# Four x tiles in the last context group, two query tiles taken singly, and V rounded in the order 3, 0, 1, 2

## What is computed

```python
q = (x @ Wq + bq)                      # x: layernormed, 1024 rows of 512; 16 heads of 32
kv = (cond @ Wkv + bkv)                # cond: 2048 rows of context
q = _fq_sym(q * scale, axis=-1)        # round(q / s) * s, s = max|q| / 127 per row and head
k = _fq_sym(k, axis=-1)
v = _fq_sym(v, axis=2)                 # s over all 2048 rows, per column: needs every context row
attn = softmax(einsum('bhqd,bhkd->bhqk', q, k))
attn = _fq_unsigned(attn, axis=-1)     # round(attn / s) * s, s = max / 255 per row
x = x + einsum('bhqk,bhkd->bhqd', attn, v) @ Wp + bp
x = x + experts(_layernorm(x))         # gate, up, down products of 8 experts
```

## Time and profile before

| | |
|---|---|
| median of 3 runs | 724.86 us |
| the profiled execution | 726.75 us, span of its instructions 724.9 us |
| granted TensorE clock, mean | 0.987 |
| DVE busy | 569.8 us, 79% |
| PE busy | 617.2 us, 85% |
| ACT busy | 462.4 us, 64% |
| POOL busy | 402.9 us, 56% |

### The profile page before, as it was taken

The page is one execution under the profiler, slowest core; times in us unless marked ns, Lnnn a source line. Parts: engine busy times, 40 slices in busy tenths (PEclk is TensorE's granted clock), DMA queues, the critical chain, the costliest instruction groups (busy, mean ns, idle before and its releaser), DMA issues.

```text
span 724.9 us, 16059 instructions
## 1 busy us (share of the span) xinstructions
PE 617.2 (85%) x5448; PEld 333.6 (46%) x5448; DVE 569.8 (79%) x927; ACT 462.4 (64%) x561; POOL 402.9 (56%) x455
## 2 busy tenths in 40 slices
PE   6999998566767777777777787799999999999995
PEld 3744444233434334443434355455555555555543
DVE  5998887999999999999999998794746547464430
ACT  5445359789979989898989896343434434353421
POOL 4164457637587878787878773315334454334503
PEclk9999999999999999999999998899999999999998
DMA  7877867999989999999999997258696797968624
GB/s 248 203 146 174 184 136 137 180 199 189 175 166 198 184 195 193 188 193 189 191 192 185 195 183 159 88 187 224 176 249 157 221 190 200 242 163 233 139 32 58
DMA packets 318517, 129.44 MB, mean 179 GB/s; under 512 B 293508, under 2 KB 293508, under 8 KB 318472
## 3 DMA queue, kind: packets, MB, share of 16 engines
q1 hardware_dynamic: 311296, 112.64, 72.6%
q0 software_dynamic: 7168, 16.26, 10.7%
q10 hardware_dynamic: 8, 0.01, 0.0%
HBM read 44.33 MB, written 12.06 MB: 78 GB/s over the span
## 4 chain that ended last, share of the span: by engine, by line
PE 38%; issue 20%; DVE 15%; POOL 8%; DMA 7%; ACT 6%; SPq 3%; POOLq 1%; another core or an unknown queue 0%; ACTq 0%; DVEq 0%
PE psum L1690 34%; DMA work<-work 6%; DVE spare L1422 5%; ACT work L1078 4%; DVE spare L1413 4%; POOL values_region L603 2%; POOL work L672 2%; SPq L481 2%; PE psum L1867 1%; POOL resid L610 1%; SPq L450 1%; PE psum L2015 1%; SPq L483 1%; POOL out_dram L846 1%; DMA token_region<-values_region 1%
## 5 line engine op out<-in xcount | busy, mean ns | idle before, releaser
L1078 ACT ACTIVATE work<-spare,exp_bias 128x2048 uint8<-128x2048 f32 (+1 forms) x127 | 253.2, 1996 | 28.3 <-POOL exp_bias L678 20.6
L1422 DVE TENSOR_SCALAR_CACHE_REDUCE spare<-psum,q_step_now 128x1024 f32<-128x1024 f32 x128 | 162.5, 1274 | 2.0 <-PE psum L1867 1.9
L672 POOL CAST work<-work 128x2048 int16<-128x2048 uint8 x70 | 132.4, 1892 | 37.9 <-DMA work<-work 33.9
L1413 DVE TENSOR_SCALAR_CACHE_REDUCE spare<-psum,q_step_now 128x2048 f32<-128x2048 f32 x64 | 150.3, 2348 | 0.1
L1867 PE MATMUL psum<-keys_region,work 128*128 128x512 f16 x256 | 72.7, 383 | 47.3 <-DVE spare L1422 27.6
L834 POOL DMA_INDIRECT work<-x_rows,slot_tok x32 | 50.9, 1591 | 86.5 <-DVE slot_w L1622 73.2
L1867 PE MATMUL psum<-keys_region,bias_hl 128*128 128x512 f16 x256 | 70.4, 381 | 28.0 <-DVE spare L1422 22.4
L846 POOL DMA_INDIRECT out_dram<-keys_region,slot_tok x32 | 51.7, 1616 | 74.7 <-ACT keys_region L1173 67.7
L1826 PEld LDWEIGHTS psum<-values_region,work 128*128 128x128 f16 x2016 | 64.8, 96 | 34.3 <-POOL work L672 20.3
L1690 PE MATMUL psum<-work,spare 128*128 128x480 f16 (+1 forms) x396 | 79.9, 362 | 0.0
L1690 PE MATMUL psum<-work,keys_region 128*128 128x480 f16 x384 | 78.9, 366 | 0.0
(11 more groups left out here) (250 smaller groups left out, 1010.4 us busy)
## 6 DMA issues: line engine op xcount, KB each, us to landing
spare<-in_L_ffn_Wd_dram SPq DMA_DIRECT2D x8, 1024.0 KB, 15.4
spare<-in_L_ffn_Wg_dram SPq DMA_DIRECT2D x7, 1024.0 KB
spare<-in_L_ffn_Wu_dram SPq DMA_DIRECT2D x7, 1024.0 KB, 10.1
work<-in_ctx_dram SPq DMA_DIRECT2D x3, 1024.0 KB, 5.8
work<-work SPq DMA_TRANSPOSE x174, 3.7
token_region<-in_L_xattn_Wkv_dram SPq DMA_DIRECT2D x2, 1024.0 KB, 7.7
resid<-in_x_dram SPq DMA_DIRECT2D x2, 1024.0 KB, 8.4
out_dram<-work SPq DMA_DIRECT2D x8, 256.0 KB, 2.6
```

What stands on the lines that cost most here:

```text
L672: nc.gpsimd.tensor_copy(p_T_int[h % 4], pair_bytes[h % 4]).then_inc(unpacked, 1)
L1078: nc.scalar.activation(p_out, scores, ACT.Exp, bias=exp_bias[:, h % 4:h % 4 + 1], scale=-1.0, accum_out=p_sum[:, h:h + 1]).then_inc(exp_do ...
L1413: nc.vector.tensor_scalar(staged[h % 4], psum[:, at:at + 4, :].rearrange("p b k -> p (b k)"), q_step_now[:, h:h + 1], None, ALU.mult, ALU.min,
L1422: nc.vector.tensor_scalar(staged[h % 4][:, 1024 * c:1024 * c + 1024], psum[:, at:at + 2, :].rearrange("p b k -> p (b k)"), q_step_now[:, h ...
```

## The change

Tiles 4 to 7 of x are now all normalised, cut and turned within the last context group, one for each key tile, alternating with the key tiles on ACT, POOL and SP. Query tiles 0 and 1 are taken by DVE singly. V's slices are rounded in the order 3, 0, 1, 2, the first two are halved by DVE and the last two by POOL, and folding the projection weights is moved behind the rounding and, for three of four columns, behind the first exponential. PE makes head 0's scores behind the fifth query product (tile 4), and the products of tiles 5 and 6 follow, that of tile 7 behind the scores of head 1. DVE stages head 0, and takes tiles 4, 5 and 6 behind it, tile 7 ahead of head 2. The `staged` buffers of the first four heads are given in another order (`FIRST_STAGED`), so that head 0 lies over V's slice 3 and head 1 over slice 2.

The diff, cut to its core:

```diff
@@ -47,6 +47,8 @@
...
+ROUNDED = (3, 0, 1, 2)
+FIRST_STAGED = (0, 2, 1, 3)
@@ -376,7 +381,9 @@
...
-                if i >= 2:
+                    if i >= KT // 2 - 2:
+                        transpose_x(2 * i + b - QT)
+                if 2 <= i < KT // 2 - 2:
@@ -409,26 +416,22 @@
...
-                if i == DK - 1:
-                    sp.wait_ge(v_rounded, DK + 1)
-                else:
-                    sp.wait_ge(v_halved, i + 1)
+                sp.wait_ge(v_halved, ROUNDED.index(i) + 1)
...
-            transpose_x(QT - 2)
-            transpose_queries(0)
-            transpose_x(QT - 1)
-            transpose_queries(1)
+            transpose_queries(0, (0,))
...
-            transpose_values(0)
-            transpose_values(1)
-            transpose_queries(2)
-            transpose_values(2)
+            transpose_values(ROUNDED[0])
+            transpose_values(ROUNDED[1])
+            transpose_queries(0, (1,))
+            transpose_values(ROUNDED[2])
+            transpose_values(ROUNDED[3])
+            transpose_queries(1)
@@ -482,9 +485,9 @@
...
-                        transpose_values(DK - 1)
-                    if first and h in (3, 4):
-                        transpose_queries(DK - 1, range(h - 3, h - 2))
+                        transpose_queries(2)
+                    if first and h < 2:
+                        transpose_queries(DK - 1, (h,))
@@ -722,10 +726,18 @@
...
+            def halve_values(n):
+                pool.wait_ge(v_rounded, n + 1)
+                pool.wait_ge(v_halved, n)
+                nc.gpsimd.tensor_copy(v_T_int[:, ROUNDED[n], :], v_i16[:, ROUNDED[n], :]).then_inc(v_halved, 1)
+
...
+            pool.wait_ge(k_cut_ready[1], KT // 2)
+            clear_queries(own, 0)
...
-            clear_queries(own, 0)
...
+            halve_values(2)
+            halve_values(3)
@@ -950,14 +966,17 @@
...
+                    if not b and not following:
+                        rows_of_x(DK + t)
...
-                    if b and not first:
-                        normalise_x(2 * g + t // 2 - 2)
-                        x_high(2 * g + t // 2 - 2)
+                    if b and following and not first:
+                        rows_of_x(2 * g + t // 2 - 2)
+                    elif b and not following:
+                        rows_of_x(DK + t)
@@ -974,17 +993,20 @@
...
-            normalise_x(QT - 2)
-
-            def round_values(i):
+
+            def round_values(n):
+                i = ROUNDED[n]
...
+
+            def fold_projection(i):
...
-            def cut_queries(i):
-                act.wait_ge(q_out, i + 1)
-                for b in range(2):
-                    if i == DK - 1 and b:
-                        act.wait_ge(q_out, DK + 1)
+            def cut_queries(i, parities=range(2)):
+                for b in parities:
+                    if i % (DK - 1):
+                        act.wait_ge(q_out, i + 2)
+                    else:
+                        act.wait_ge(q_out, i + i // 2 + b + 1)
@@ -996,21 +1018,17 @@
...
-            act.wait_ge(wp_in, 16)
...
-            x_high(QT - 2)
+            cut_queries(0, (0,))
...
-            normalise_x(QT - 1)
-            cut_queries(0)
-            x_high(QT - 1)
-            round_values(2)
-            cut_queries(1)
+            cut_queries(0, (1,))
...
+            round_values(2)
...
-            cut_queries(2)
-            act.wait_ge(v_rounded, DK)
-            nc.scalar.activation(v_T_int[:, DK - 1, :], v_i16[:, DK - 1, :], ACT.Copy).then_inc(v_rounded, 1)
+            act.wait_ge(wp_in, 16)
+            fold_projection(0)
+            cut_queries(1)
@@ -1055,7 +1073,13 @@
...
-                        cut_queries(DK - 1)
+                        for c in range(1, DK):
+                            fold_projection(c)
+                        cut_queries(2)
+                    if first and 1 <= h < 3:
+                        cut_queries(DK - 1, (h - 1,))
+                    if first and h < DK:
+                        act.wait_ge(v_halved, ROUNDED.index(h) + 1)
@@ -1348,22 +1374,20 @@
...
-            def halve_values(i):
-                dve.wait_ge(v_rounded, i + 1)
+            def halve_values(n):
+                dve.wait_ge(v_rounded, n + 1)
...
-                nc.vector.tensor_copy(v_T_int[:, i, :], v_i16[:, i, :]).then_inc(v_halved, 1)
-
-            query_tiles(0, 0, 2)
-            halve_values(0)
-            query_tiles(1, 2, 2)
+                nc.vector.tensor_copy(v_T_int[:, ROUNDED[n], :], v_i16[:, ROUNDED[n], :]).then_inc(v_halved, 1)
+
+            query_tiles(0, 0, 1)
+            query_tiles(1, 1, 1)
...
+            halve_values(0)
...
-            halve_values(2)
-            query_tiles(2, 4, 2)
-            query_tiles(3, 6, 1)
-            base = head + query_steps * (DK + 1)
+            query_tiles(2, 2, 2)
+            base = head + query_steps * (DK + 2)
@@ -1434,11 +1464,15 @@
...
+                    if first and h == 2:
+                        make_bias(i, 1)
+                        query_tiles(5, QT - 1, 1)
...
-                        query_tiles(DK, QT - 1, 1)
-                    if first and h:
+                        query_tiles(3, 4, 2)
+                        query_tiles(4, 6, 1)
+                    if first and h > 2:
@@ -1877,21 +1911,24 @@
...
-                    queries(QT - 1)
+                    for t in range(DK + 1, QT - 1):
+                        queries(t)
...
-                    if first and h == 6:
-                        pe.wait_ge(q_out, DK + 1)
+                    if first and h == 2:
+                        pe.wait_ge(q_out, DK + 2)
...
-                        if head % 2 == 0:
+                        if head % 2 == 0 and (h or not first):
...
+                    if first and h == 0:
+                        queries(QT - 1)
...
```

More of the change, by code:

```diff
@@ L266, in bank, with stage_home @@
             return psum[:, b, :]
+        def stage_home(h, first):
+            return staged[FIRST_STAGED[h] if first and h < 4 else h % 4]
         ctx_in, small_in, wq_in, wp_in = (sem(n) for n in ("ctx_in", "small_in", "wq_in", "wp_in"))
@@ L598, in row, with keys_low @@
                 return resid[:, bass.ds(j, 1), :].rearrange("p a d -> p (a d)")
-            def keys_low(j):
-                for b in range(2):
+            def keys_low(j, parities=range(2)):
+                for b in parities:
                     pool.wait_ge(k_hi, 2 * j + b + 1)
@@ L622, in _ @@
             pool.wait_ge(small_in, 64)
-            with pool.Fori(2, QT) as j:
+            with pool.Fori(2, KT // 2 - 2) as j:
                 keys_low(j)
                 x_low(j - 2)
-            x_low(QT - 2)
-            x_low(QT - 1)
+            for j in range(DK, QT):
+                keys_low(KT // 2 - 2 + (j - DK) // 2, (j % 2,))
+                x_low(j)
             pool.wait_ge(x_biased, QT)
@@ L936, in _, with rows_of_x @@
             take_first(2)
+            def rows_of_x(j):
+                normalise_x(j)
+                x_high(j)
             def key_group(g, following, first=False):
@@ L1073, in attention_tile @@
                         act.wait_ge(unpacked, unpacked_by(i, 9))
-                    scores = staged[h % 4] if words else staged[h % 4].rearrange("p (c k) -> p c k", c=2)
+                    scores = stage_home(h, first)
+                    if not words:
+                        scores = scores.rearrange("p (c k) -> p c k", c=2)
                     p_out = p_words[h % 4] if words else p_bytes[h % 4]
@@ L1402, in stage_ready @@
                     dve.wait_ge(exp_done, H * i + h - 3)
+                if first and h == 0:
+                    dve.wait_ge(v_rounded, 1)
+                if first and h == 1:
+                    dve.wait_ge(v_rounded, DK)
                 if first and h == 3:
                     dve.wait_ge(wp_ready, DK)
+                if first and h == 5:
+                    dve.wait_ge(exp_done, 3)
                 if not first and h % HQ == 0:
@@ L1412, in stage_whole @@
                 at = h % 4
-                nc.vector.tensor_scalar(staged[h % 4], psum[:, at:at + 4, :].rearrange("p b k -> p (b k)"), q_step_now[:, h:h + 1], None, ALU.mult, ALU.min,
+                nc.vector.tensor_scalar(stage_home(h, first), psum[:, at:at + 4, :].rearrange("p b k -> p (b k)"), q_step_now[:, h:h + 1], None, ALU.mult, ALU.min,
                                         accum_out=s_low[:, h % 4:h % 4 + 1]).then_inc(scores_taken, 2)
@@ L1422, in stage_half @@
                 nc.vector.tensor_scalar(
-                    staged[h % 4][:, 1024 * c:1024 * c + 1024], psum[:, at:at + 2, :].rearrange("p b k -> p (b k)"),
+                    stage_home(h, first)[:, 1024 * c:1024 * c + 1024], psum[:, at:at + 2, :].rearrange("p b k -> p (b k)"),
                     q_step_now[:, h:h + 1], None, ALU.mult, ALU.min,
@@ L1793, in queries @@
                 add_bias(bank(Q_BANKS[t % 4]), 1).then_inc(q_full, 1)
-            for t in range(QT - 1):
```

(3 more changed lines are left out.)

4 lines of the change are left out of this document (2 added, 2 removed).

## The result

The changed kernel takes 727.93 us (median of 9 runs, 725.74 to 733.99), the kernel before in the same comparison 722.37 us (9 runs). The ratio is 1.0063, with a 95% interval of 1.0037 to 1.0089: 2.7 to 6.4 us slower, 4.5 in the middle (the two medians lie 5.6 us apart, inside that interval). Measured a second time, beside the experiments, it is 1.0038 (1.0009 to 1.0067), 2.7 us. The forecast was +1.1 us. All ratios of this document leave out executions that took over 1.5% longer than the fastest one of the same kernel: two of the kernel before (1574.10 and 3347.56 us), one of the x part alone (729.50) and one of tiles 0 to 3 ahead with PE kept busy (1029.09).

What follows compares the result with a forecast made beforehand. DVE was taken to set attention's pace, so only head 2's start on DVE counted: +1.35 us from the steps, less 0.12 and 0.15, gave +1.1 on 724.86, or 726.0 us. The range was 724.0 to 728.2.

Steps and rivals of the forecast that it cites:

- Steps 1 and 2: ACT and SP at the front: V's rounding starts 0.8 us later, at 106.3; query tile 0 lands at 112.5.
- Step 3: SP's transposing queue: four V slices at 2.45 us and two query tiles take 12.5 us; tile 2 lands at 125.0.
- Without a gap: SP's queue: the six transfers behind query tile 0 follow each other directly, each ready when its turn comes.
- Step 4: ACT's own list ends at 123.5, the cut of tile 4 waits until 125.0; ACT alone only 1.4 us earlier.
- Rival A: ACT bound: V's transfers cheaper, cut of tile 4 starts 1.4 us earlier; 0 to -0.8, kernel at 724.5; chance 0.20.
- Step 6: DVE's step of tile 7 meets POOL's last L733: 0 to 1.0 us, taken as 0.8; head 2 at 132.1.
- corrections: Taken off head 2's +1.35: 0.12 for head 1's bias made earlier, 0.15 for steps coming out 0.25 late in old order.
- Attention passes the shift on: From head 2 to the end: DVE does not rest in attention, so all of +1.1 us reaches the kernel's time.
- Rival B: Queue starts late through slower transposes beside the weight load or ACT's last group: +2 to +3.5, kernel at 727.6; chance 0.20.
- Rival C: Early staging of head 0 pays, tile 4's cut not late: head 2 -2.9 or -1.5, kernel 722 to 723.4; chance 0.14.

Runs made afterwards that it cites:

- the x part alone: Kernel before with only the four last x tiles normalised, cut and turned within the last context group, query and V work as before: ratio 0.9978.
- tiles 0 to 3 ahead with PE kept busy: Changed kernel with query tiles 0 to 3 ahead of V slices 1 and 2 in SP's order, plus throwaway matmuls in PE's idle time: ratio 1.0039.
- tiles 2 and 3 ahead of two slices: Changed kernel with query tiles 2 and 3 ahead of the last two V slices in SP's order, tile 1 still behind the first two: ratio 1.0023.
- tiles 0 to 3 ahead: Changed kernel with SP's order alone changed: query tile 1 behind tile 0, tiles 2 and 3 ahead of V slices 1 and 2: ratios 0.9980, 0.9991.
- tiles 0 to 5 ahead: Changed kernel with SP's order tiles 0 and 1, V slice 3, tiles 2 and 3, slices 0 and 1, tiles 4 and 5, slice 2: 0.9983, 0.9986.

## Why the prediction came out as it did

The direction and the mechanism up to head 2 were right; the size at the end was too small, and the step from head 2 to the end is not confirmed. That 727.93 us lies in the range of 724.0 to 728.2 is partly luck: the kernel before stood at 722.37 in that comparison and not at the 724.86 on which the range was built, and 1.0063 of 724.86 would be 729.4, outside. Step by step, the measured times with 1.42 added:

| step | predicted | measured |
|---|---|---|
| first V rounding | 106.3 | 105.96 |
| tile 0 landed | 112.5 | 112.1 |
| head 0 staged | 115.1 | 115.3 |
| tile 2 landed, cut of tile 4 starts | 125.0 | 125.7 |
| DVE's wait before tile 6 | 3.7 | 3.80 |
| head 1 | 126.75 | 127.6 |
| head 2 | 132.1 | 132.7 |

- **Steps 1 and 2** came 0.35 to 0.4 early. The key transpose beside the weight load took 4.4 us, a little less than the 4.7 assumed, and x tile 6 landed behind it. Counted from the first query product the rounding started 0.46 us later than before in the first execution (0.8 was predicted) and at the old place in the second (6.49 against 6.46).
- **Step 3** is the term of the sum that was mis-sized. Tile 0 to tile 2 took 124.25 - 110.7 = 13.6 us, not 12.5. One landing follows the last by 3.1 (V slice 3), 3.2 (slice 0), 0.9 (tile 1), 2.1 (slice 1), 2.9 (slice 2) and 1.4 us (tile 2): the slices cost 2.8 in the mean, where the earlier trace rows gave 2.45, and the two query tiles 2.2 together instead of 2.8. "Without a gap" was also not quite so: DVE took query tile 1 first and finished halving slice 3 at 109.10, so SP issued it at 109.28, 0.49 us behind the end of the issue before it. By the Trainium skill's rate (DMA: Bandwidth & Descriptors, latency and other measured facts) the six would be an estimated 10 us, further off still.
- **Step 4**: ACT's idle before the cut was 1.51 for the predicted 1.4. Rival A needed this to be 0, and it was 1.50 in the second execution as well.
- **Step 6**: the meeting with POOL cost 0.3 (0.48 for L1366 against 0.18), not 0.8. The reading behind it, that DVE's step is not held up by L732, rested on one place. In the changed kernel the same instruction (now L744) does hold it up, to its own end:

```profile
117.61 0.38 DVE L1366 TENSOR_SCALAR scratch<-row_scales 128x32 f32<-128x32 f32 x1
```
```profile
116.38 1.58 POOL L744 TENSOR_SCALAR spare<-spare,v_fold 128x512 f32<-128x512 f32 x1
```

- **Head 2** came 1.4 to 2.0 us later than before, in the mean 33.50 - 31.82 = 1.7, for the +1.35 of the steps, from which 0.27 had been taken off as corrections. The second of these, 0.15, is a part of a deviation of 0.25 for which the prediction gives no reason.
- **"Attention passes the shift on"** is the step that the runs leave open. The heads follow at the old distance but for waits on PE's scores, and these are in the kernel before as well. But the time grew by 2.7 to 4.5 us (the two middles) for 1.7 us at head 2, and against the kernel before every order of the changed kernel ends worse than its head 2 says: by 2.0 us in the changed kernel itself, 2.0 with tiles 2 and 3 ahead of two slices, 0.4 with tiles 0 to 3 ahead, 1.2 with tiles 0 to 5 ahead. The ratios are uncertain by 1.3 to 2.1 us either way, so these point to a small cost behind head 2 without sizing it, and no run isolates it. Single traces can't find it: the time from head 2 to the end is 594.0 to 595.0 us in three executions of the kernel before, 595.3 and 597.1 in two of the changed one, and 591.2 to 597.1 over all kernels here. The order of V's slices, their halving on POOL and the order of the staging buffers were not tested apart.
- **Rival B** (a slow start) had the nearest time, 727.6, and the wrong mechanism: the rounding came no later than step 1 had it, and the x part alone costs nothing that can be measured.
- **Rival C** is what the changed kernel becomes with another queue order: DVE works on from head 0, head 2 starts 2.0 to 2.6 us earlier than before (2.9 in the rival), and 1.0 to 1.2 us seem to arrive at the end.

## What to carry to other kernels

Work moved to the front of a queue that one engine issues in order is paid for by what it pushes back: list every transfer that a waiting instruction now stands behind, and put the one that an engine waits for ahead of the one that is only ready. Here that order alone took away a loss of 2.7 to 4.5 us, and perhaps gained one more. Before a difference between two traces is explained, take a second trace of each kernel: here both the late start of the one and the fallen clock of the other would have been put down to the change. And do not let one instant stand for the rest: a kernel whose head 2 started 0.3 us earlier than before was still 1.7 us slower by its ratio.

## What the runs showed of the hardware

- The granted clock is not a property of the kernel: the same program had 1.00 from 99 to 430 us in one execution and 0.72, 0.71 and 0.73 in three stretches of 6 us in another, that is 1.2 GHz for part of each. With it eight score matmuls took 3.44 us in the changed kernel instead of 2.08 (two groups of four at 1.04). DVE's waits on scores go from 1.9 to 3.6 us in the kernel before; no difference of the median could be tied to it.
- A V slice on the transposing queue has no fixed price: the four landed 3.1, 3.2, 2.1 and 2.9 us behind the transfer before them in the changed kernel. In the kernel before the other two slices, not read for the prediction, landed 2.6 and 2.3 behind (issued at 121.08 and 122.95, landing 5.1 and 5.5 later, behind a query tile at 123.5), so its 2.45 was typical there and still too low for the new order. A price read in one order of a queue deserves a wider range in another.
- DVE's step instruction (L1340, later L1366) takes 0.18 us, and 0.38 to 0.63 over these traces where it meets some of POOL's: it then ends within 0.05 us of POOL's instruction. Beside POOL's `TENSOR_SCALAR` on 128x512 it ran freely when it started 0.58 us after it (126.99 against 126.41 in the kernel before) and was held when it started 1.23 us after it (117.61 against 116.38 in the changed one).
